# Conv columns ordered by block, with the eight samples side by side, in a quantised conv and dense kernel

## The reference

```
c  = conv1d(x, weight, 9 taps, pad 4, groups=4) + ctx[:, :, None] + bias[None, :, None]
xq = fake_quant(c, 8 bits, axis=-1)        # scale = max|row| / 127, round
kq = fake_quant(kernel, 8 bits, axis=0)
y  = einsum('bsd,df->bsf', xq, kq) + fake_quant(bias, 16 bits)
out = x + fake_quant(y, 8 bits, axis=-1)
```

## Time and profile before

| what | value |
|---|---|
| median of 3 runs | 251.21 us (251.17 to 253.18) |
| the profiled execution's own time | 252.55 us |
| its span, first to last instruction | 250.5 us |
| mean granted TensorE clock | 0.982 |
| PE busy | 235.4 us, 94% |
| DVE busy | 206.7 us, 83% |
| POOL busy | 191.0 us, 76% |
| ACT busy | 184.2 us, 74% |

### The profile page before, as it was taken

One profiled execution on the slowest core, in us unless ns is written; L12 is line 12 of the kernel. 1 busy time (PEld: TensorE's weight loads), 2 busy tenths in 40 slices (PEclk: granted clock), 3 DMA queues, 4 the chain that ended last, 5 costly groups with the idle time before them and its releaser, 6 DMA issues.

```text
span 250.5 us, 3993 instructions
## 1 busy us (share of the span) xinstructions
PE 235.4 (94%) x1314; PEld 151.0 (60%) x1314; DVE 206.7 (83%) x421; ACT 184.2 (74%) x183; POOL 191.0 (76%) x135
## 2 busy tenths in 40 slices
PE   7789999999999999999999999999999999999920
PEld 4568667756666666666656666665666666656400
DVE  4689897775898888778997898989798989877894
ACT  4569788785887777758688859876988875966652
POOL 4572451309999999897849994997899599989980
PEclk9799999999999999999999999999999999999995
DMA  7996724011307899989798989999999998968928
GB/s 214 396 413 251 268 82 158 12 74 48 123 0 155 184 245 267 314 185 236 168 319 233 217 216 293 260 188 321 239 253 308 279 375 167 280 117 231 413 110 334
DMA packets 15716, 56.03 MB, mean 224 GB/s; under 512 B 1744, under 2 KB 1872, under 8 KB 15696
## 3 DMA queue, kind: packets, MB, share of 16 engines
q1 hardware_dynamic: 11664, 41.82, 45.8%
q0 software_dynamic: 3744, 13.63, 30.7%
q10 hardware_dynamic: 288, 0.33, 0.4%
HBM read 39.00 MB, written 16.78 MB: 223 GB/s over the span
## 4 chain that ended last, share of the span: by engine, by line
PE 88%; DVE 6%; DMA 2%; issue 1%; ACT 0%; SPq 0%; DVEq 0%
PE dense_ps L676 41%; PE conv_ps L620 36%; PE turn_ps L656 6%; PE small_ps L646 2%; DMA xwin<-x_windows 2%; PE dense_ps L698 1%; DVE a_int L911 1%; DVE y_max L937 1%; DVE small_ps L882 1%; PE dense_ps L689 1%; PE conv_ps L676 1%; DVE y L877 1%; DVE last_max L962 0%; DVE k_max L834 0%; ACT x_hi L432 0%
## 5 line engine op out<-in xcount | busy, mean ns | idle before, releaser
L676 PE MATMUL dense_ps<-kq,a_t 128*128 128x512 bf16 x496 | 115.5, 379 | 0.0
L316 POOL TENSOR_TENSOR x_lo<-xwin,x_hi 128x1032 fp32r<-128x1032 f32 x32 | 81.9, 2571 | 31.6 <-ACT x_hi L432 26.0
L324 POOL TENSOR_TENSOR y<-y,bq 128x512 f32<-128x512 f32 x60 | 81.2, 1440 | 11.7 <-DVE y L868 11.7
L676 PEld LDWEIGHTS dense_ps<-kq,a_t 128*128 128x128 bf16 x496 | 47.2, 100 | 49.0 <-issue 2.0
L882 DVE TENSOR_REDUCE small_ps<-conv_ps 128x8 f32<-128x1024 f32 x32 | 39.2, 1227 | 18.4 <-PE conv_ps L620 18.4
L471 ACT CAST a_t<-turn_ps 128x1024 bf16<-128x1024 int16 x32 | 32.3, 1010 | 23.6 <-PE turn_ps L656 23.4
L486 ACT ACTIVATE y_int<-y,y_inv 128x1024 int16<-128x1024 f32 x31 | 35.6, 1148 | 18.2 <-DVE y_inv L923 18.1
L868 DVE SCALAR_TENSOR_TENSOR y<-dense_ps,row_scale,k_scale_b 128x512 f32<-128x512 f32 x58 | 43.1, 744 | 6.1 <-PE dense_ps L676 5.8
L620 PE MATMUL conv_ps<-x_hi,w_hi 128*128 128x512 f32 x128 | 40.2, 436 | 1.6 <-ACT x_hi L432 1.6
L911 DVE TENSOR_TENSOR a_int<-conv_ps,inv 128x1024 int16<-128x1024 f32 x32 | 39.2, 1224 | 0.2 <-DVE inv L903 0.2
L937 DVE TENSOR_REDUCE y_max<-y 128x1 f32<-128x1024 f32 x31 | 37.4, 1208 | 0.0
(11 more groups left out here) (67 smaller groups left out, 156.8 us busy)
## 6 DMA issues: line engine op xcount, KB each, us to landing
xwin<-x_windows SPq DMA_DIRECT2D x32, 516.0 KB, 6.1
out<-y SPq DMA_DIRECT2D x30, 512.0 KB, 4.9
y<-x_rows POOLq DMA_DIRECT2D x26, 512.0 KB, 7.7
k_raw<-ffn_kernel SPq DMA_DIRECT2D x8, 512.0 KB, 8.1
x_sb<-x_rows SPq DMA_DIRECT2D x6, 512.0 KB, 7.1
w_raw<-taps SPq DMA_DIRECT2D x2, 256.0 KB, 3.3
b_row<-ffn_bias SPq DMA_DIRECT2D x1, 512.0 KB, 9.8
out<-x_sb SPq DMA_DIRECT2D x1, 512.0 KB, 3.1
```

What stands on the lines that cost most here:

```text
L316: pool.tensor_tensor(x_lo[:, at].rearrange("p n b -> p (n b)"), xwin[:, t % XWIN, :], x_hi[:, at].bitcast(F32).rearrange("p n b -> p (n b) ...
L324: pool.tensor_tensor(y[:, t % YRING, half(h)], y[:, t % YRING, half(h)], bq[:, half(h)], ALU.add).then_inc(s["biased1" if h else "biased_e ...
L676: mm = pe.matmul(dense_bank(t, h), a_t[:, t % LEVELS, q].rearrange("b j o -> b (j o)"), kq[:, q, half(h)], start=(q == 0), stop=(q == Q - 1))
```

## The change

The columns of the convolution are ordered block by block, with the eight samples side by side in each block, in place of sample by sample. The host lays the windows out that way, `x_hi` and `x_lo` get the shape `[WIN, NS]`, and the accumulator is read and written as 128 blocks of 8 samples. The half `hs` of a matmul is now 64 blocks of all eight samples (`BH`), not four samples (`NH`), and its 512 columns are one run. `a_int` keeps its layout, a sample's 128 blocks next to each other, since the transposes read it so. `column_max` therefore reads the accumulator with a step of 8 elements, 128 of them for each sample, and `levels` reads it in one run and writes each 16-bit level 128 elements (256 bytes) after the one before it, for eight samples, and then goes on to the next block.

No instruction is added, removed or moved on any engine. The bytes of every transfer are as many as before.

```diff
-NH = HALF // BLOCKS
+BH = HALF // NS
...
-        x_hi = sb("x_hi", [P, XSPLIT, NS, WIN], F32R)
-        x_lo = sb("x_lo", [P, XSPLIT, NS, WIN], F32R)
+        x_hi = sb("x_hi", [P, XSPLIT, WIN, NS], F32R)
+        x_lo = sb("x_lo", [P, XSPLIT, WIN, NS], F32R)
...
         def conv_cols(at):
-            return conv_ps[:, at].rearrange("p h (n b) -> p (h n) b", b=BLOCKS)
+            return conv_ps[:, at].rearrange("p h (b n) -> p (h b) n", n=NS)
...
-                act.copy(conv_cols(t % 2), ctx_cols[:, g, n0:n0 + NS].unsqueeze(2)
-                         .to_broadcast([P, NS, BLOCKS])).then_inc(s["seeded"], 1)
+                act.copy(conv_cols(t % 2), ctx_cols[:, g, n0:n0 + NS].unsqueeze(1)
+                         .to_broadcast([P, BLOCKS, NS])).then_inc(s["seeded"], 1)
...
                             mm = pe.matmul(
-                                conv_ps[:, at, hs, :].rearrange("p (n b) -> p n b", n=NH),
+                                conv_ps[:, at, hs, :],
                                 w[:, ch, g].rearrange("p q o -> p (q o)"),
-                                x[:, x_at, hs * NH:(hs + 1) * NH, ch:ch + BLOCKS],
+                                x[:, x_at, hs * BH + ch:(hs + 1) * BH + ch, :].rearrange("p b n -> p (b n)"),
                                 start=False, stop=False, skip_group_check=True)
...
                 dve.tensor_reduce(cmax_ps,
-                                  conv_ps[:, t % 2].rearrange("p h (n b) -> p (h n) b", b=BLOCKS),
+                                  conv_cols(t % 2).rearrange("p b n -> p n b"),
                                   AX_X, ALU.max, apply_absolute_value=True
                                   ).then_inc(s["col_max_made"], 1)
...
-                dve.tensor_tensor(a_int[:, at, :].rearrange("p (n b) -> p n b", b=BLOCKS),
+                dve.tensor_tensor(a_int[:, at, :].rearrange("p (n b) -> p b n", b=BLOCKS),
                                   conv_cols(at),
-                                  inv8[:, at].unsqueeze(2).to_broadcast([P, NS, BLOCKS]),
+                                  inv8[:, at].unsqueeze(1).to_broadcast([P, BLOCKS, NS]),
                                   ALU.mult).then_inc(s["a_rounded"], 1)
...
-    windows = padded.reshape(N // NS, NS, GROUPS, CG, WIN, Q)[..., ::-1].transpose(0, 2, 5, 3, 1, 4)
+    windows = padded.reshape(N // NS, NS, GROUPS, CG, WIN, Q)[..., ::-1].transpose(0, 2, 5, 3, 4, 1)
```

More of the change, by code:

```diff
@@ L315, in split @@
                 at = t % XSPLIT
-                pool.tensor_tensor(x_lo[:, at].rearrange("p n b -> p (n b)"),
+                pool.tensor_tensor(x_lo[:, at].rearrange("p b n -> p (b n)"),
                                    xwin[:, t % XWIN, :],
-                                   x_hi[:, at].bitcast(F32).rearrange("p n b -> p (n b)"),
+                                   x_hi[:, at].bitcast(F32).rearrange("p b n -> p (b n)"),
                                    ALU.subtract).then_inc(s["lo_made"], 1)
@@ L431, in round_x @@
                 wait(act, "lo_made", t - XSPLIT + 1)
-                act.copy(x_hi[:, t % XSPLIT].rearrange("p n b -> p (n b)"),
+                act.copy(x_hi[:, t % XSPLIT].rearrange("p b n -> p (b n)"),
                          xwin[:, t % XWIN, :]).then_inc(s["hi_made"], 1)
@@ L828, in _ @@
                     dve.wait_ge(s["ctx_made"], 1)
-                    dve.tensor_copy(conv_cols(0), ctx_cols[:, 0, 0:NS].unsqueeze(2)
-                                    .to_broadcast([P, NS, BLOCKS])).then_inc(s["seeded_first"], 1)
+                    dve.tensor_copy(conv_cols(0), ctx_cols[:, 0, 0:NS].unsqueeze(1)
+                                    .to_broadcast([P, BLOCKS, NS])).then_inc(s["seeded_first"], 1)
             def k_maximum(fb):
@@ L1089 @@
     arrays = {
-        "x_windows": windows.reshape(TILES, P, NS * WIN),
+        "x_windows": windows.reshape(TILES, P, WIN * NS),
         "x_rows": x.transpose(0, 2, 1, 3, 4).reshape(TILES, P, L),
```

## The result

The changed kernel took 341.75 us as the median of four runs (340.56 to 342.48), the kernel before 251.19 us beside it. The ratio is 1.357, 95% interval 1.352 to 1.363: slower, by 91 us and not by 13.

The account below looks back on a forecast made before the run. PE was taken to bound the kernel, DVE second. DVE's 1.0 us more a tile gave +7 long stretch, +5 early, +0.5 tail: +12.5 on 251.21 us, forecast 264 us, range 245 to 277; PE's 7.5 us gain unseen.

Parts of the forecast that it names:

- The bound and the direction: PE sets the pace, DVE second with about 1 us slack a tile; slower likeliest (0.54), forecast 264 us.
- rival A: Both DVE steps, L882 and L911, cost about 0.5 us more: 255 to 272 us, the forecast; chance 0.32.
- rival C: Only the L911 write costs, about 0.5 us: 247 to 250 with PE's gain (0.16), 251 to 254 without (0.11).
- The price of the levels (L911): DVE's stepped 16-bit write of `a_int`: 0.5 us more for each `levels`, taken from L806, a stepped read.
- the upper bound: For L911: POOL's 2.49 ns an element, making `levels` 2.55 us, 1.3 more.
- the prediction's own way of adding: Extra DVE time over 32 tiles, less about 28 us of DVE's waits, gives the time added.
- The lower bound: For L911: no extra cost, by ACT's copy L471, said to read runs of 16 and write in another order.
- The price of the column maximum (L882): DVE's accumulator read 8 elements apart: 0.5 us more for each, from L806's step price.
- The slack: DVE's waits, 21.8 us long stretch, 5.8 early: half stay lost at worst; middle values +7 and +5 us.
- The conv matmuls: PE at L620: one run of columns saves up to 20 ns each, 7.5 us in all; full gain 0.6 likely.
- The cover of the seed: ACT's seed L441 costs nothing; were it 0.5 us dearer, 41 us of idle ACT time would cover it.
- rival B: The L911 write costs 1.3 us, the L882 read 0.5: 283 us, range 275 to 295; chance 0.10.

Follow-up runs that it names:

- e7: The changed kernel, with `levels` still jumping 256 bytes but writing two neighbouring 16-bit levels at each landing; 250.2 us, ratio 0.9917 to the kernel before.
- second probe: The kernel before with operations on scratch at its start, GpSimd kept still; lone 16-bit writes 512 bytes apart took 4708 ns; no kernel time given.
- e6: The kernel before plus two unused DVE reductions of 400 accumulator columns for each tile; 253.94 us, ratio 1.009.
- e5: The changed kernel with `a_int` as 4-byte integers, written 512 bytes apart, transposes reading the lower halves; 253.4 us, ratio 1.005 to the kernel before.
- e1: The changed kernel with the loop order of `levels` turned back: stepped accumulator read, `a_int` written in one run; 250.96 us, ratio 0.9942 to the kernel before.

## Why the prediction was wrong, step by step

**The bound and the direction held.** PE set the pace, DVE was next with about 1 us of slack a tile, and the change turned that over: rival A's mechanism, DVE in the chain, its waits for the conv gone, PE waiting at L656. That the direction came right is luck in part: with its own 0.5 us for L911 and the nothing that L882 turned out to cost, the prediction would have been at its rival C, 247 to 254 us. It was the size of the error that made the kernel slower.

**The price of the levels (L911) was mis-sized, and this is the failed step.** The prediction took 0.5 us and bounded it by 1.3. It is 3.56 us. Two things went wrong. The nearest row, L806, is a read of 4-byte elements; the write here was of 2-byte elements, and the probes show these as different things (1.9 against 4.7 us). And the upper bound was a rate of another engine on another pattern, POOL's 2.49 ns an element in one run. It bounds nothing about a pattern that no row has. With the measured price, the prediction's own way of adding gives 32 × 3.56 = 114 us, less 27.6 us of waits (21.8 and 5.8), so 337 us for the span, against 338.8. Two differences nearly cancel in that: DVE is busy 105.6 us longer and not 114, and its idle time falls by 17.3 us and not by 27.6.

The lower bound was misread too. L471 reads in one run and writes runs of 16 elements of 2 bytes, 256 bytes apart, not the other way round. It was a row of a stepped write, in runs, at no extra cost (1010 ns), and fits e7; it says nothing of lone elements.

The Trainium skill, "Vector Engine (DVE) Microarchitecture Reference", section 5.2, pointed the right way: lone writes are dear. Its 1.71 ns a column for a hop at every element is near what the 4-byte write had here, 1.90 us for 1024 [second probe], but its figures are for 4-byte streams, and the estimate from them (0.67 to 1.48 us more) was too low by more than half for 16-bit levels. The measurement decides. Even so it stood above the 0.5 us taken for a write from the row of a read.

**The price of the column maximum (L882) was wrong the other way.** 0.5 us predicted, nothing measured (1213 ns, and 1224 in the probe for the accumulator's memory). L806's price is real for SBUF, 1.89 us in the second probe, but the accumulator is another memory, as the prediction noted and then did not weigh.

**The slack** isn't shown wrong. The prediction let up to half of DVE's waits go unused and took the middle. By the same working e6, with 16.8 us more of DVE in the long stretch against 21.8 us of waits, comes to nothing if all of them can be used, to 5.9 us if half are lost, so to 3 in the middle; the early stretch (3.1 us against 5.8) adds next to nothing. Measured were 2.3 us (1.2 to 3.3). e5 agrees: 21.4 us more of busy time and 1.1% against e1. So the waits took up most of a dose smaller than they are, and losing half in full is ruled out for such a dose. For the 32 us that the prediction took, more than the 27.6 us of waits, there is no run. An estimate from 32 - 27.6 us at the least and from the prediction's own sum at the most is 256 to 264 us, had both prices been as taken.

**The conv matmuls.** The gain is real and small: 0.05 us for 12, where 0.24 was hoped for. The 0.6 for the full gain was too much; the row ends have 4 of the 20 ns. By the Trainium skill, "SBUF — State Buffer", the note on cachelines, long rows should be free, and that was nearly so. e1 and e7, which keep the new columns and in which L911 and L882 take what they took before, give 0.6% and 0.8%, about what 384 times 4 to 5 ns, 1.5 to 1.9 us, would be.

**The cover of the seed** held: L441 took 1015 ns in its new order.

**The range** left out rival B, the dear write, which had the right kind of cause, and even B stopped at 295 us. Two small slips in the rivals change nothing: B's own terms give 58 less 28, so 30 us and not 32, and C with PE's gain adds up to 247 to 249 us, not 250. The text had named the case, "wrong on the high side if L911 goes beyond 2 us", with no price behind it.

## What to carry to other kernels

When a layout change makes one side contiguous, look at the element size and the memory of the side that becomes stepped. Here a stepped read of the accumulator was free on DVE and ACT, a stepped 4-byte write of SBUF took half as much time again (probe) to two thirds (e5), and lone 2-byte writes took nearly four times the time; turning the loop so that the step falls on the read, or writing in aligned pairs, removed all of it and left a kernel 0.6 to 0.8% faster than the one before. A bound for a pattern that no row shows has to be said to be open. And a dose is measured by what it adds to the engine's busy time, not by the durations of the instructions put in: here 0.73 and not 1.13 us a tile.

## What the runs showed of the hardware

- Lone 16-bit writes to SBUF at steps of 16 bytes or more take 4.6 ns each on VectorE (4.69 us for 1024 at 16 bytes, 4.71 at 512, 4.70 for bf16 and 4.70 with a source in the accumulator's memory), and 4.6 ns on ScalarE too (4.73 us).
- Whole 4-byte words written alone take 1.9 ns each 16 or 512 bytes apart and 1.2 ns 8 bytes apart; two neighbouring 16-bit elements that fill a word take 2.4 ns together, as in one run.
- Reads of the accumulator's memory 32 or 512 bytes apart take the time of one run (1224 ns for 1024).
- A matmul train with 4-byte columns 8 bytes apart takes 457 ns for 512 columns (12 of them from 23.21 to 28.69 us), nearly twice the 232 ns of one run.
